# Decoder-layer kernel on one NeuronCore: the third layer norm applied by ScalarE for all four batches

## What is computed

```
x = x + attn(layernorm(x))              # scores reshaped by bands of their sigmoid, softmax, projection
x = x + xattn(layernorm(x), ctx, ctx)   # 8 heads, decay matrix from cumulated log-sigmoid gates, group norm
x = x + ffn(layernorm(x))               # 256 -> 1024 -> 256, gelu, and a low-rank term made of tokens 1..16

def _layernorm(x, eps=1e-05):
    return (x - mean(x)) / sqrt(var(x) + eps)
```

## Time and profile before

| | |
|---|---|
| median of 3 runs | 1824.24 us (1824.04 to 1824.56) |
| the profiled execution, its own time | 1826.38 us |
| its span, first to last instruction | 1824.7 us |
| PE busy | 1738.5 us, 95% |
| PEld busy | 1380.1 us, 76% |
| DVE busy | 1377.1 us, 75% |
| ACT busy | 1172.4 us, 64% |
| POOL busy | 395.0 us, 22% |
| mean granted TensorE clock | 0.983 of full |
| one step in the loop | 53.45 us |

### The profile page before, as it was taken

One profiled execution on the slowest core, in us unless ns is written; L12 is line 12 of the kernel. 1 busy time (PEld: TensorE's weight loads), 2 busy tenths in 40 slices (PEclk: granted clock), 3 DMA queues, 4 the chain that ended last, 5 costly groups with the idle time before them and its releaser, 6 DMA issues.

```text
span 1824.7 us, 47628 instructions
## 1 busy us (share of the span) xinstructions
PE 1738.5 (95%) x15708; PEld 1380.1 (76%) x15708; DVE 1377.1 (75%) x4092; ACT 1172.4 (64%) x2666; POOL 395.0 (22%) x330
## 2 busy tenths in 40 slices
PE   5669999999999999999999999999999999999897
PEld 4557777788777777877777877777787777778676
DVE  4677777878777887877778777778787777877752
ACT  1457766666676666667666676766667676666552
POOL 2012222221222222122222212222212222221220
PEclk8879999999999999999999999999999999999998
DMA  5111212221121222121122112122211212221100
GB/s 140 35 38 38 61 38 61 61 60 38 47 60 39 61 61 58 32 55 50 49 61 61 55 31 60 40 59 61 60 51 34 61 38 61 61 60 38 26 16 27
DMA packets 226879, 93.05 MB, mean 51 GB/s; under 512 B 154896, under 2 KB 226320, under 8 KB 226848
## 3 DMA queue, kind: packets, MB, share of 16 engines
q1 hardware_dynamic: 226848, 92.65, 19.6%
HBM read 70.84 MB, written 16.78 MB: 48 GB/s over the span
## 4 chain that ended last, share of the span: by engine, by line
PE 90%; DVE 5%; issue 2%; ACT 1%; SPq 1%; DMA 0%; DVEq 0%; ACTq 0%
PE UA L1490 12%; PE TA L1490 6%; PE GT L1490 6%; PE UB L1428 5%; PE TB L1428 5%; PE PV L1428 5%; PE GT L1502 3%; PE TA L1390 3%; PE QQ L1253 3%; PE UA L1453 3%; PE UA L1428 2%; PE DD L1253 2%; PE PV L1543 2%; PE QQ L1528 2%; PE UB L1543 2%
## 5 line engine op out<-in xcount | busy, mean ns | idle before, releaser
L1124 DVE TENSOR_TENSOR C<-qT,QKs 128x512 f32<-128x512 f32 x256 | 176.7, 711 | 124.2 <-ACT qT L774 121.3
L1490 PE MATMUL UA<-W2f,hs_all 128*128 128x256 f32 x1024 | 236.3, 379 | 0.0
L1490 PEld LDWEIGHTS UA<-W2f,hs_all 128*128 128x128 f32 x1024 | 194.4, 190 | 30.4 <-issue 0.2
L594 POOL TENSOR_TENSOR ot<-xg,b_b 128x1024 f32<-128x1024 f32 x32 | 76.3, 2385 | 552.4 <-DMA out<-ot 500.2
L625 POOL TENSOR_TENSOR Ng<-HT,gnw_b 128x256 f32<-128x256 f32 x128 | 93.3, 729 | 440.1 <-DVE cden L1137 435.5
L619 POOL TENSOR_TENSOR xg<-x,gnb_b 128x1024 f32<-128x1024 f32 x32 | 75.5, 2359 | 305.4 <-DVE Evl L1116 288.2
L1490 PE MATMUL TA<-W2f,hs_all 128*128 128x256 f32 x512 | 126.0, 379 | 0.0
L1490 PE MATMUL GT<-W2f,hs_all 128*128 128x256 f32 x512 | 115.8, 379 | 0.0
L691 ACT ACTIVATE V<-QQ 128x260 f32<-128x260 f32 x32 | 12.4, 388 | 159.5 <-PE QQ L1285 159.5
L755 ACT ACTIVATE QKs<-DD 128x512 f32<-128x512 f32 x64 | 38.3, 598 | 102.3 <-PE DD L1453 102.3
L1490 PEld LDWEIGHTS GT<-W2f,hs_all 128*128 128x128 f32 x512 | 94.8, 190 | 11.7
(11 more groups left out here) (392 smaller groups left out, 5350.9 us busy)
## 6 DMA issues: line engine op xcount, KB each, us to landing
xin<-x SPq DMA_DIRECT2D x32, 512.0 KB, 4.4
xb<-x SPq DMA_DIRECT2D x32, 512.0 KB, 4.1
blocks<-ctx SPq DMA_DIRECT2D x256, 64.0 KB, 2.0
vc<-ctx SPq DMA_DIRECT2D x32, 512.0 KB, 3.6
out<-ot SPq DMA_DIRECT2D x32, 512.0 KB, 3.2
Ev<-xn SPq DMA_DIRECT2D x256, 4.0 KB, 1.7
hs_all<-L_ffn_W SPq DMA_DIRECT2D x4, 512.0 KB, 8.9
E<-xn SPq DMA_DIRECT2D x128, 16.0 KB
```

The lines of the kernel that those rows point to most:

```text
L594: pool.tensor_tensor(ot[:, :, :], x3[:, :, :], b2_b[:, :].unsqueeze(1).broadcast_to([P, G, D]), ALU.add).then_inc(xf_ok.h, 1)
L1124: dve.tensor_tensor(C[:, b % 2, :, half], dx[hf].rearrange("p (h i) -> p h i", h=HEADS), QKs[:, b, :, half], ALU.mult)\
L1490: ins = pe.matmul(OB[b][:, 0:D], hs_all[:, k, b * S:(b + 1) * S], W2f[:, k, :], start=(i == 0), stop=(i == KH - 1))
```

## The change

ScalarE applies the third norm to all four batches, VectorE to none. The counter `xn3_ok` is raised once per step instead of twice, and who waits for it waits for one. VectorE's three waits in front of its part go with it; the same three stand in `apply_third` already.

```diff
-        xn_ok = [per_step("xn1_ok", COMING, 1), per_step("xn2_ok", SELF, 1), per_step("xn3_ok", CROSS, 2)]
+        xn_ok = [per_step("xn1_ok", COMING, 1), per_step("xn2_ok", SELF, 1), per_step("xn3_ok", CROSS, 1)]
...
             def e_rows(it):
 
                 sp.wait_ge(e_ok.h, e_ok.at(it, 1))
-                sp.wait_ge(xn_ok[2].h, xn_ok[2].at(it, 2))
+                sp.wait_ge(xn_ok[2].h, xn_ok[2].at(it, 1))
...
             def apply_third(it):
...
                 act.wait_ge(nmr3_ok.h, nmr3_ok.at(it, 1))
-                for b in range(G // 2, G):
+                for b in range(G):
                     ins = act.activation(xn3[:, b, :].rearrange("p (c u) -> p c u", c=CB),
                                          x3[:, b, :].rearrange("p (u c) -> p c u", c=CB), ACT.Identity,
                                          bias=nmr3[:, b:b + 1], scale=rs[:, 2, b:b + 1])
...
                 if cross:
                     dve.scalar_tensor_tensor(nmr3[:, :], mean[:, 2, :], -1.0, rs[:, 2, :], ALU.mult, ALU.mult)\
                        .then_inc(nmr3_ok.h, 1)
-                    dve.wait_ge(xn3T_mm.h, xn3T_mm.at(it, 2))
-                    dve.wait_ge(e_loaded.h, e_loaded.at(it, 0))
-                    dve.wait_ge(ev_loaded.h, ev_loaded.at(it, 2 * R * 16))
-                    ln_apply(2, x3, xn3, range(G // 2))
                 if own:
                     dve.wait_ge(xn2T_mm.h, xn2T_mm.at(it, 2))
                     ln_apply(1, x2, xn2)
```

## The result

| | before | after |
|---|---|---|
| median | 1824.4 us of 4 runs (1824.04 to 1825.13) | 1876.02 us of 4 runs (1875.28 to 1877.15) |
| ratio | | 1.0283, 95% interval 1.0267 to 1.0298 |
| the profiled execution, its own time | 1826.38 us | 1875.28 us |
| its span | 1824.7 us | 1873.6 us |
| one step in the loop | 53.45 us | 54.93 us |

The change makes the kernel slower by 51.6 us. The forecast was 1873.4 us, with a range of 1859 to 1880.

The account below looks back on a forecast made before the run. TensorE, busy 95% of the span, was taken to bound the kernel. Delays of 29 x 1.54 and 3 x 1.51 us summed to 49.2 us, so 1824.24 + 49.2 = 1873.4 us, range 1859 to 1880.

Parts of the forecast that it names:

- ScalarE gets two activations more: At the third norm, ScalarE's four activations take 3.11 us instead of 1.60, so xn3 is complete 1.51 us later.
- The sum of 31.6 us: Loss if each further activation of the third norm took the skill's 0.49 us, which knows no stride: 32 x 0.99.
- All of the delay lies on the path: TensorE's transposes of xn3 start later by the whole delay: 1.54 us per loop step, 1.51 in 3 end steps.
- between 0.12 and 0.22: Wake-up in us from ScalarE's end to TensorE's transposes: 0.12 seen in the loop, 0.22 in step 32, where TensorE waits.
- the wait and register instructions that fall away: Queue instructions the change removes; claimed worth zero, since they stand in queues that are waiting there.
- an interval of 0.12 us is therefore no slack at all: Before the change, ScalarE's half of the norm just arrives as TensorE gets to the transposes of xn3.
- No return: After the transposes, all engines move together and the hole at L1453 absorbs nothing, so none of the delay comes back.
- stand where they stood: SyncE's copies and store move 1.51 us, just as the step does, so nothing shifts relative to their users.
- part is given back: Rival: the hole at L1453 closes as VectorE reaches its scan earlier; up to 13.8 us returns, 1860 us, 7%.
- VectorE loses two operations: VectorE saves 0.85 us a step at the third norm, then idles until Z; claimed worth nothing.
- The clock: Rival: the hole at the transposes costs TensorE full clock in each loop step, 1.43 us each, 1915 us; 5%.
- The rival of "faster": VectorE is what the step waits for, so its saved 0.85 us comes off each step, 27 us, 1797 us; 2%.

Follow-up runs that it names:

- e4: Changed kernel with ScalarE's four activations read and written without a stride, so its result differs; 1843.55 us, ratio 1.0104.
- e1: Kernel before, with the third norm split one batch on VectorE and three on ScalarE; 1851.33 us, ratio 1.0146.
- e9: Kernel before, with GpSimd's addition into xb held back until VectorE's scan L1045 is done; 1846.19 us, ratio 1.0118.
- e12: Kernel before, with GpSimd's addition to xb put ahead of its operation on vc; 1818.97 us, ratio 0.9963.
- e3: Changed kernel, with VectorE still doing its two old operations, into a spare tile nobody reads; 1876.7 us, ratio 1.0281.
- e5: Changed kernel, same regrouping, but ScalarE reads in order and writes with the stride; 1862.11 us, ratio 1.0199.
- e6: Changed kernel, with two more ScalarE activations into a spare tile ahead of the four; 1951.03 us, ratio 1.069.
- e15: Changed kernel, but with all four batches of the third norm on VectorE and none on ScalarE; 1828.29 us, ratio 1.0018.
- e2: Kernel before, with three batches of the third norm on VectorE and one on ScalarE; 1812.98 us, ratio 0.9934.
- e16: e2, with SyncE's block of copies also waiting until TensorE's last low-rank product is done; 1830.06 us, ratio 1.0028.
- e7: Changed kernel, with twelve transposes of the identity into a free bank ahead of the real ones; 1871.54 us, ratio 1.0255.

## Why the prediction was right, and where it was off

**ScalarE gets two activations more.** Predicted 3.11 us for the four, measured 3.06; a further one took 0.74 us, not 0.756. ScalarE's busy time rose by 49 us, not by the 54 that was named as a sign: 64 x 0.844 counts the overlap of neighbours twice. The 0.52 us for a further activation without a stride was a quarter of the row; less the first one's 0.59 us it is 0.49. That is also the prediction's estimate by the Trainium skill (ScalarE: Activation LUTs, "What ACT_TABLE_LOAD costs"), and e4, without the stride, shows 0.50. The sum of 31.6 us that rested on it is no run's: in e4 all four are without a stride, and the loss is 18 us.

**All of the delay lies on the path.** Right in its size, since both ways start at the norm's end, which came 1.46 us later where 1.51 was predicted. Predicted at the transposes was 1.54 us, measured 1.57. The wake-up of "between 0.12 and 0.22" was no matter of a busy or a waiting TensorE. In the loop it is 0.13 us in before, e1, e9 and e12, in e1 with TensorE standing still; step 32, from which the 0.22 us to the weight load was read the earlier trace rows, has two instructions in the queue, and so have the changed kernel, e3, e4, e5, e6 and e15 in the loop, with 0.24. That "the wait and register instructions that fall away" are worth zero is therefore not right: they moved a wait behind the norm's, 0.11 us on TensorE and 0.05 on SyncE. And the transposes are not what the step waits for last: "an interval of 0.12 us is therefore no slack at all" holds for their start, but L1453 had 0.45 us in hand.

**No return.** This step failed, in a small size. The hole at L1453 does not "absorb nothing": it takes up 0.08 us of the 1.57. That SyncE and GpSimd, relative to their users, "stand where they stood" is not true to 0.1 us either: SyncE starts 0.16 us ahead of the transposes where it was 0.10. TensorE lost 0.11 us to its queue and SyncE 0.05, and the step follows SyncE. Of the 1.57 us, 1.49 is left, about 2.3 us over the loop. So the rival "part is given back" was there, worth 2 us and not 13.8, and by a path that I had not seen: I wrote that the return needs VectorE to start early, and it is SyncE that does. e2 and e16 show that this path is worth 12 to 17 us a run when it moves by 0.35 to 0.67 us.

**VectorE loses two operations: worth nothing.** Right: e3.

**The clock.** I gave it 5%, as all steps or none. It was neither: 2 of 28 steps, at 1.24 us each, a little under my price of 1.43. The row at 53.45 that spoke against it had a gap of 1.34 us, and the experiments with 1.37 us and less agree with it; the hole that came was 1.81 us, wider than any that the trace of before had in the loop. The Trainium skill's page on the gate (TensorE: Matmul & The Clock Gate, "A second HAM failure mode"), where short idle stretches in an iteration make the clock oscillate, describes e6, with 23 of 28 steps, better than the changed kernel with its 2.

**The sum.** 29 x 1.54 + 3 x 1.51 = 49.2 us was the forecast. The profiled execution was predicted at 1875.6 us and took 1875.28. There the shorter activations (-), the wake-up (+), the return (-), the falls of the clock (+), the longer slow stretch ahead of the loop (+), a shorter delay in the last step and the tail (-) nearly cancel, so the last digit is luck. The largest of them, the falls with 2.5 us, stood in the sum at nothing. Between the medians the loss is 51.6 us, 2.4 more than forecast, since the profiled execution of before lay 2 us above its median and the one of after 0.7 us below. The likeliest range of 1870 to 1877 us held both.

**The rival of "faster".** None in this direction; but e2 shows that the change of the split in the other direction is faster, for a reason that the prediction's sentence on SyncE denied.

## What to carry to other kernels

Divide shared work by when each engine ends against the moment the consumer can take it, not by busy shares: here two engines ended 0.93 and 0.12 us ahead of it, and the slower per item got more. When an operation's end releases several queues, follow each of them to where they meet again: being early is free on one and pays on another, as the store and GpSimd showed. A wait that is moved in the code can put one more instruction between a release and the work, 0.11 us here. And if a short operation's duration is many times its least, look for what GpSimd does at its end.

## What was not expected of the hardware

- A VectorE operation of 0.17 to 0.41 us took 0.74 to 2.40 us beside a GpSimd addition, and ended with it (e9: 2.40 us for one that takes 0.21). Moving the GpSimd operation moved the loss to the VectorE operations that met it (e9), or made it smaller (e12).
- The same regrouping by a stride costs an activation of 128x256 fp32 in a row 0.24 us on the read and 0.10 on the write.
- One hole in each step of some 55 us: up to 1.37 us no fall of the granted clock was seen in the loop, at 1.81 us 2 or 3 in 28 steps, at 3.27 us 23. A fall costs 1.2 us. Why at 1.81 us it is these steps and not others stays open.
- From the norm's end to the first weight load of the transposes it is 0.12 us with one instruction in TensorE's queue between them (the loop in before, e1, e7, e9 and e12) and 0.23 with two (the changed kernel, e3, e4, e5, e6 and e15; a few steps 0.28). How long TensorE had stood still didn't matter: 0 to 0.7 us in the loops of the first group, 0.1 to 3.0 in the second. In the last three steps of e7, with none between them, it is 0.05.
